# Eight DMA clears of expert regions, issued in a row ahead of the row loads that they alternated with (post-norm attention and mixture-of-experts layer, one core)

## The reference

```python
x = _layernorm(x + _L0_attn_ref(x, w_qkv, w_conv1))

# _L0_ffn_ref, xf is [4096, 256], E = 8 experts, K = 2 of them for a token, H = 192
scores = softmax(xf @ gate_w.T)
top_vals, top_idx = top_k(scores, K)
w_dense = zeros((T, E)).at[arange(T)[:, None], top_idx].set(top_vals)
h = einsum('td,ehd->teh', xf, W1)
y, g = split(h, 2, axis=-1)
eo = einsum('teh,edh->ted', y * silu(g), W2)
z = einsum('te,ted->td', w_dense, eo) + _gated_mlp(xf, Ws1, Ws2)

x = _layernorm(x + z)
```

## Time and profile before

| | |
|---|---|
| time before, median of 3 runs | 360.88 us |
| the three runs | 360.88, 361.18, 356.59 us |
| the profiled execution's own time | 360.88 us |
| its span, first to last instruction | 359.0 us |
| mean granted TensorE clock | 0.962 |
| PE busy | 317.5 us (88%) |
| DVE, ACT, POOL busy | 261.2, 192.0, 197.9 us (73%, 53%, 55%) |
| DMA | 54.65 MB, mean 152 GB/s |

### The profile page before, as it was taken

The page is one execution under the profiler, slowest core; times in us unless marked ns, Lnnn a source line. Parts: engine busy times, 40 slices in busy tenths (PEclk is TensorE's granted clock), DMA queues, the critical chain, the costliest instruction groups (busy, mean ns, idle before and its releaser), DMA issues.

```text
span 359.0 us, 7811 instructions
## 1 busy us (share of the span) xinstructions
PE 317.5 (88%) x2241; PEld 283.4 (79%) x2241; DVE 261.2 (73%) x1037; ACT 192.0 (53%) x425; POOL 197.9 (55%) x223
## 2 busy tenths in 40 slices
PE   4799899999999999899988999999999998999700
PEld 2366788789888888888788989999989998989600
DVE  2884779665989887664667766676668968958876
ACT  1043777744547372733315555565655557757673
POOL 4058748736578755557170453444755765665530
PEclk9969999899999999999999999999999999999955
DMA  7967426502021213513024545444899886888667
GB/s 230 370 227 245 118 62 155 138 26 78 30 91 62 92 64 99 149 61 108 16 107 123 166 151 151 120 133 132 178 258 199 215 199 168 192 219 248 185 222 301
DMA packets 31384, 54.65 MB, mean 152 GB/s; under 512 B 4880, under 2 KB 22544, under 8 KB 31344
## 3 DMA queue, kind: packets, MB, share of 16 engines
q1 hardware_dynamic: 23136, 29.82, 28.3%
q0 software_dynamic: 8208, 24.32, 23.9%
HBM read 29.73 MB, written 24.40 MB: 151 GB/s over the span
## 4 chain that ended last, share of the span: by engine, by line
PE 39%; issue 17%; DVE 11%; DMA 11%; SPq 9%; POOL 6%; ACT 3%; another core or an unknown queue 2%; DVEq 0%; POOLq 0%
PE bank L1048 12%; PE bank L1070 7%; PE bank L932 6%; DMA stage<-ws_t 3%; PE bank L1017 3%; PE bank L954 3%; SPq L408 3%; PE bank L1057 3%; DMA stage<-rows_in 3%; PE bank L917 2%; SPq L409 2%; POOL rows_in L555 2%; POOL w1lo L509 2%; DMA rows_out<-stage,place 2%
## 5 line engine op out<-in xcount | busy, mean ns | idle before, releaser
L592 POOL DMA_INDIRECT rows_out<-stage,place x71 | 69.2, 975 | 70.5 <-ACT stage L759 55.2
L555 POOL DMA_INDIRECT rows_in<-x,slot x64 | 65.3, 1020 | 43.5 <-DVE slot L1268 26.9
L759 ACT ACTIVATE stage<-bank,weight 128x256 f32<-128x256 f32 x71 | 29.8, 471 | 23.5 <-PE bank L1070 18.9
L1048 PE MATMUL bank<-w1hi,xthi 128*128 x142 | 39.2, 357 | 1.5 <-issue 1.5
L742 ACT ACTIVATE stage<-bank 128x384 f32<-128x384 f32 (+1 forms) x36 | 17.5, 487 | 41.0 <-PE bank L1048 25.9
L1048 PE MATMUL bank<-w1lo,xthi 128*128 x142 | 36.3, 336 | 0.0
L1048 PE MATMUL bank<-w1hi,xtlo 128*128 x142 | 36.2, 336 | 0.0
L1370 DVE TENSOR_TENSOR xtlo<-bank,xthi 128x512 fp32r<-128x512 f32 (+1 forms) x36 | 24.3, 678 | 15.1 <-ACT xthi L687 11.6
L1497 DVE TENSOR_TENSOR stage<-bank,stage 128x384 f32<-128x384 f32 (+1 forms) x36 | 19.8, 550 | 20.1 <-ACT stage L742 14.3
L679 ACT ACTIVATE mix<-bank 128x512 f32<-128x512 f32 x24 | 14.1, 589 | 35.8 <-PE bank L932 35.2
L932 PE MATMUL bank<-xthi,ws1hi 128*128 128x512 f32 x96 | 31.8, 413 | 0.7 <-DVE mix L1353 0.7
(11 more groups left out here) (242 smaller groups left out, 892.5 us busy)
## 6 DMA issues: line engine op xcount, KB each, us to landing
stage<-rows_in SPq DMA_DIRECT2D x71, 133.0 KB
xs<-rows_out POOLq DMA_DIRECT2D x12, 512.0 KB
xs<-x SPq DMA_DIRECT2D x8, 512.0 KB, 8.3
out<-xs SPq DMA_DIRECT2D x7, 512.0 KB
stage<-w_t SPq DMA_DIRECT2D x8, 384.0 KB, 4.9
rows_in<-clear SPq DMA_DIRECT2D x16, 133.0 KB
rows_out<-stage,place POOLq DMA_INDIRECT x71
stage<-w_t SPq DMA_DIRECT2D x2, 512.0 KB, 3.9
```

The source lines that it names most:

```text
L555: pool.indirect_dma_start(rows_in[0:E * CAP, :], bass.IndirectOffsetOnAxis(slot[:, q * G + t, k:k + 1], 0), x2[q % 2][:, t, :], None).then ...
L592: pool.indirect_dma_start(rows_out[:, :], bass.IndirectOffsetOnAxis(place[:, 2 * j + b:2 * j + b + 1], 0), by[j % 4][:, b * C:(b + 1) * C] ...
L759: ins = act.activation(by[j % 4][:, b * C:(b + 1) * C], result_bank(j)[:, b * C:(b + 1) * C], ACT.Copy, scale=weight[:, j // 2 % 2, at_w:a ...
L1048: mm = pe.matmul(bank_h[j % 2][:, b, 0:F], bx[j % 2][:, (2 * b + k) * P:(2 * b + k + 1) * P], w[:, bass.ds(e, 1), k, :], start=(a == 0), s ...
```

## The change

The 8 clears, which stood two and two behind the loads of pairs 4, 5, 6 and 7, now stand together ahead of the load of pair 4, right behind the wait for `s_ends`. Their number, addresses and sizes are the same, as are all waits and the order of the loads among themselves. All other engines' programs are unchanged apart from line numbers, which move up by one behind line 424.

```diff
             for j in range(4):
                 load_rows(j)
             sp.wait_ge(s_ends, 1)
-            share_of = E // (FULL // 2 - 4)
+            for e in range(E):
+                r = sp.value_load(zrow[0:1, e:e + 1], min_val=0, max_val=ROWS - P)
+                sp.dma_start(rows_in[bass.ds(r, P), :], clear[:]).then_inc(s_pad, 16)
             for j in range(4, FULL // 2):
                 load_rows(j)
-                for e in range((j - 4) * share_of, (j - 3) * share_of):
-                    r = sp.value_load(zrow[0:1, e:e + 1], min_val=0, max_val=ROWS - P)
-                    sp.dma_start(rows_in[bass.ds(r, P), :], clear[:]).then_inc(s_pad, 16)
             for n in range(2):
                 sp.wait_ge(s_sc[n], 16 * K * G * NP)
             sp.wait_ge(s_pad, 16 * (IDLE + E))
```

## The result

| | before | after |
|---|---|---|
| median | 360.77 us (17 runs, 356.59 to 363.93) | 362.52 us (17 runs, 360.81 to 364.15) |
| ratio | | 1.0086, 95% interval 1.0063 to 1.0108 |
| span of the profiled execution | 359.0 us | 362.9 us |
| its mean granted TensorE clock | 0.962 | 0.966 |

The change makes the kernel 0.9% slower. It was forecast at 0.3% faster. The profiled execution of the change took 364.79 us, 2.3 more than its median, so its trace shows more than the typical loss.

What follows compares the result with a forecast made beforehand. PE's own work was taken to bound the pair loop, except at pair 8, held by the last clear. From 360.88 us, 1.07 us go and the moved clears add zero, giving 359.8 us, range 355.4 to 361.8.

Steps and rivals of the forecast that it cites:

- What bounded the kernel before: Pair loop: PE's own work bounds; SP counts only at pair 8, whose load the last clear made 1.07 us late.
- the term: PE's wait at pair 8: gain between 0.80 us (idle time) and 1.07 us (the step's excess), taken as 1.07.
- The removed part: Clears leave 191.00 to 207.04 us; pair 8's load lands at 208.6, 3.9 us before PE wants it.
- The failed step: Behind the region ends: 8 clears at 1.13 us each fit SP's idle time until 187.15, so cost zero.
- the 1.6 from which PE would have seen it: Early clears on SP: each would have to cost 1.6 us before PE saw it at pair 4.
- a late pair 4: Rival at 178 to 190 us: queued clears and scatters delay pair 4's rows, PE waits 3.3 us; 363.1 us, chance 0.06.
- The DMA engines' share: At 178 to 187 us, scatters and clears together: share 0.65 and 211 GB/s, under the sustained 0.77, costed zero.
- a lag of 0.4 us in the clears: Beside POOL's scatters: SP's clears get half the engines, 115 GB/s against 120 asked, 0.4 us behind after 8 clears.
- The lost gain: Rival: the time won at pair 8 is lost later, candidate pair 20's load; 360.9 us, chance 0.14 including an unchanged wait.
- The split of the runs: Rival over whole runs: the median falls on the lower kind, like the 356.59 us run; 355.5 us, chance 0.16.
- The range: Whole kernel's time, 8 in 10: 355.4 to 361.8 us, spanning the two likeliest cases and most of the lower kind.

Runs made afterwards that it cites:

- the second trace of before: The unchanged kernel before, run once more beside the change in the same session: 361.10 us in its one run.
- e2: Kernel before plus 8 small transfers (16 floats a row, with register reads) at the early clears' place: 0.9996 without the slow stretch, 1.0065 with it.
- e8: Kernel before plus 8 register reads and no transfer at the early clears' place, real clears unmoved: ratio 1.0038.
- The hold: POOL waits ahead of the 5th of its last 8 scatters for PE's pair 0 first-layer signal: on kernel before 0.9975, on the change 0.9909 and 0.9884.
- the first session: First runs of four variants against the kernel before, on a chip without the slow stretch: kernel before 353.6 us, ratios 0.9976, 0.9996, 1.0027, 0.9983.
- e3: Kernel before plus one transfer of 8 x 133 KB at the early clears' place, real clears unmoved: 1.0027 without the slow stretch, 1.0022 with it.
- e1: Kernel before with 4 clears ahead of pair 4's load, 4 one each behind loads of pairs 4 to 7: 0.9976 without the slow stretch, 1.0061 with it.

## Why the prediction was wrong, point by point

- **What bounded the kernel before** was read rightly as far as it went: pair 8 was late by 1.07 us because of the last clear, and the change took that away (21.2 against 22.3 us from pair 3 to pair 8, 1.1). But the second trace of before shows no such wait, since PE came to pair 8 late by its clock. The wait is there only when PE is on time, so the term is an upper end and not a constant.
- **The removed part**: right in its effect. No trace with the early clears waits at pair 8.
- **The failed step** is "I therefore cost the moved issues at nothing: the cover is SP's own idle time". SP's own time cost nothing, as forecast, though not by the forecast numbers: a clear took 1.53 us and not 1.13, under the 1.6 from which PE would have seen it; SP was free at 191.5, the places of quad 0 came at 191.2, and pair 4's rows were in time for PE. What I didn't ask was who else suffers while SP works at 178 to 187 us. I bounded the price above by a late pair 4, since "nothing on PE's path reads from DRAM before 195.92"; PE's path needs no DRAM there, but it needs PE's own signals to come through to DVE and ACT. The stretch from the region ends to pair 3 took 3.5 us more in the profiled execution (1.8 of it the lower clock behind the idle time), where the prediction had put zero. In the medians the whole change, this loss less the gain at pair 8, is 1.75 us slower.
- **The sign was in the rows of before.** ACT waited 8.61 us ahead of a SiLU whose input PE had finished at 185.3, 4.4 us earlier. A wait that outlasts its releaser's work by this much points at something else; I should have asked what, right where the change put its work.
- **The DMA engines' share** was forecast at 0.65 and 211 GB/s; the windows of 2 us from 180 to 186 us show 0.55 to 0.71 and 196 to 251. Over the 178 to 187 us of the forecast they show 0.46 and 162, since the clears were spread over 12.3 us. It stayed under the 0.77 and wasn't what mattered. The Trainium skill (DMA: Bandwidth & Descriptors, Queues, rings and completion order) let me expect a lag of 0.4 us in the clears from engines that take turns between queues; e2 and e8 show the delay of PE's signals with few bytes and with none, which that rule doesn't speak of. No view of these runs shows how the DMA engines took turns between the two queues.
- **The rivals.** Slower by a late pair 4: not in the change; in the kernel with the clears on POOL it cost 0.86 us. The lost gain: in the first pair of traces pair 20's wait grew from 0.34 to 1.11 us, which is most of what pair 8 had won; in the second it was 0.86 before and 0.59 after. So it varies between executions and isn't shown to follow from the change. The split of the runs: the three runs' spread was real (356.6 to 363.9 over 17), the changed kernel's is narrower (360.8 to 364.2) and lies in the upper half of that. That fits a delay which the change makes certain and the kernel before has in part; it was not shown for single runs.
- **The range** (355.4 to 361.8) missed by 0.7 us. It held no bound for what SP's work does to others.

## What stays open

The hold shows that POOL's unbroken run of scatters is needed for the delay: broken in two, ACT's SiLU comes 4 us earlier, with the clears beside it. It isn't enough for it: in the first session the run was unbroken and the SiLU came at 8.2 us. In single traces the register reads and the issues on SP each add to the delay of DVE's addition. By which path scatters, SP's instructions and PE's signals get into each other's way, no view shows. Nor is it known why one session had none of it, or whether its chip is the reason. The delay is also only a part of what sets that session apart: the kernel before is 6 to 10 us faster in it, while its two traces with the clears in their old places (e2, e3) have pair 8 at 34.3 and 34.9 us instead of 35.8 and 36.2. The change itself wasn't run there, so whether it gains there is open; e1, e2 and e3, which came out 0.2 to 0.65% slower elsewhere, cost nothing there that could be measured. A shorter or longer hold, or one in the groups before, wasn't tried.

## What to carry to other kernels

Issues moved into a queue's idle time can cost that queue nothing and others something, as here. Look at what every other engine waits for in that stretch, and take a wait that lasts longer than its releaser's work as a warning that something else already holds that stretch up. And where two edits act on the same chain, one ahead of a pinned transfer and one on the transfer, try them together: here one lost 0.9%, the other came out 0.25% faster, not clear of no change, and both together won about 1%.

## What the runs showed of the hardware

- With 8 indirect scatters of 128 rows in a run on POOL, what PE finished in the first 2 us of the run reached ACT at once (178.60 and 180.50 us in the changed kernel), and what it finished from 5 us on reached DVE and ACT late. In the changed kernel DVE acted 6.4 us late and ACT 4.5 us late, ACT when the last scatter had landed by estimate. Single checks of a register on SP took up to 0.71 us, where the median was 0.02. A break of 2.4 to 2.7 us after the 4th scatter removed this (first SiLU at 7.5 to 7.8 instead of 11.9 us).
- The same kernel took 353.6 us on one chip and 359.5 to 363.3 on three others, one session each. The traces of the first, of close relatives of that kernel, are without this delay.
- After 5 us in which PE was idle the granted clock was 0.50 for the next 3 to 4 us: 3.91 instead of 2.09 us for 12 pieces. In the second trace of before, idle stretches of 0.97 and 1.83 us came ahead of the same fall: 3.54 us.
